# Softmax probabilities turned in 32x32 blocks on VectorE and spread by SBUF to SBUF transfers, in place of TensorE transposes, in a two-block attention kernel

## What is computed

```python
# block 0, q = x, k = v = ctx
qn, kn, vn = _ln(q, ...), _ln(k, ...), _ln(v, ...)
qh, kh, vh = (einsum('btd,hed->bhte', n, W) for n, W in ((qn, Wq), (kn, Wk), (vn, Wv)))
attn = einsum('bhte,bhse->bhts', qh, kh) + rel_bias[idx]
p = softmax(attn / sqrt(HS), axis=-1)
out = einsum('bhts,bhse->bhte', p, vh)
x = q + out.reshape(B, T, H * HS) @ fc_w.T + fc_b
x = x + gelu(_ln(x, ln2_g, ln2_b) @ W1.T + b1) @ W2.T + b2
# block 1, query = x, key = value = ctx
scores = where(|i - j| <= 64, q @ k.T / sqrt(16), NEG)
attn = (softmax(scores) @ v) @ Wo + bo
gate = silu(concat([attn, query]) @ Wg + bg)
out = attn * gate + query * (1 - gate)
x_hat = out * rsqrt(mean(out * out) + EPS) * rms_w
return x_hat - mean(x_hat, axis=1)
```

## Time and profile before

| what | value |
|---|---|
| median of 3 runs | 2212.92 us |
| the profiled execution | 2203.2 us |
| its span, first to last instruction | 2201.5 us |
| PE busy | 2152.8 us, 98% |
| PE weight loads (beside PE) | 1978.8 us, 90% |
| VectorE busy | 1575.8 us, 72% |
| ScalarE busy | 1648.2 us, 75% |
| POOL busy | 891.0 us, 40% |
| mean granted TensorE clock | 0.997 of full speed |
| DMA | 37.36 MB, 32236 packets |

### The profile page before, as it was taken

How to read it: one execution, slowest core, us unless ns; L and a number is a source line. 1 busy time by engine, 2 the same in 40 slices (tenths; PEclk the granted TensorE clock), 3 DMA queues, 4 the chain that set the end, 5 groups by cost and what they waited for, 6 DMA issues and landing times.

```text
span 2201.5 us, 57835 instructions
## 1 busy us (share of the span) xinstructions
PE 2152.8 (98%) x20908; PEld 1978.8 (90%) x20908; DVE 1575.8 (72%) x6779; ACT 1648.2 (75%) x5742; POOL 891.0 (40%) x978
## 2 busy tenths in 40 slices
PE   8999999999999999999999999999999999999985
PEld 8998999999999999999999999999999999999973
DVE  4666777767777767777777777777777776777764
ACT  3677787777787777787777787777777787777774
POOL 1234444434444434444434344434444433444433
PEclk9999999999999999999999999999999999999998
DMA  5000000000000000000000000000000000000000
GB/s 174 11 11 11 16 9 16 14 12 15 16 9 16 14 16 11 16 9 16 14 16 11 16 9 16 14 16 11 16 9 16 14 16 11 16 9 16 4 6 10
DMA packets 32236, 37.36 MB, mean 17 GB/s; under 512 B 2512, under 2 KB 30800, under 8 KB 31952
## 3 DMA queue, kind: packets, MB, share of 16 engines
q1 hardware_dynamic: 31952, 33.67, 4.9%
HBM read 25.27 MB, written 8.39 MB: 15 GB/s over the span
## 4 chain that ended last, share of the span: by engine, by line
PE 96%; DVE 1%; ACT 1%; issue 0%; DMA 0%; POOL 0%; SPq 0%; POOLq 0%; DVEq 0%; ACTq 0%
PE bank L276 20%; PE bank L277 19%; PE bank L278 19%; PE bank L416 6%; PE bank L439 6%; PE bank L536 6%; PE bank L426 5%; PE bank L284 3%; PE bank L549 3%; PE bank L526 3%; PE bank L577 2%; PE bank L357 1%; PE bank L292 1%; PE bank L360 1%; ACT soft L1852 1%
## 5 line engine op out<-in xcount | busy, mean ns | idle before, releaser
L2232 POOL TENSOR_TENSOR soft<-soft,inv_sum 128x512 f32<-128x512 f32 x256 | 266.7, 1042 | 443.9 <-DVE inv_sum L1227 441.5
L1852 ACT ACTIVATE soft<-soft,row_min 128x128 f32<-128x128 f32 x1024 | 396.4, 392 | 48.9 <-DVE row_min L1219 48.7
L1774 ACT ACTIVATE soft<-soft,row_min 128x128 f32<-128x128 f32 x1024 | 398.5, 393 | 34.8 <-DVE row_min L1099 34.0
L2224 POOL TENSOR_TENSOR soft<-soft,inv_sum 128x512 f32<-128x512 f32 x256 | 268.6, 1049 | 268.1 <-DVE inv_sum L1107 264.4
L1099 DVE CUSTOM_DVE_ANT_0 soft<-bank,relb 128x128 f32<-128x128 f32 x1024 | 232.6, 282 | 14.6 <-PE bank L416 12.3
L1219 DVE CUSTOM_DVE_ANT_0 soft<-bank,winb 128x128 f32<-128x128 f32 x1024 | 224.4, 284 | 13.1 <-PE bank L526 13.1
L1852 ACT ACTIVATION_READ_ACCUMULATOR soft<-soft,row_min 128x1 f32 x1024 | 195.4, 191 | 0.0
L1774 ACT ACTIVATION_READ_ACCUMULATOR soft<-soft,row_min 128x1 f32 x1024 | 195.0, 190 | 0.0
L1077 DVE TENSOR_SCALAR kT<-bank,bk 128x256 f32<-128x256 f32 x256 | 111.1, 474 | 106.9 <-PE bank L278 106.7
L1764 ACT ACTIVATE qT<-bank,bq 128x256 f32<-128x256 f32 x256 | 106.2, 467 | 107.1 <-PE bank L278 106.3
L536 PE MATMUL bank<-ident,soft 128*128 128x128 f32 x1024 | 160.3, 280 | 6.2 <-POOL soft L2232 6.2
(11 more groups left out here) (197 smaller groups left out, 7581.7 us busy)
## 6 DMA issues: line engine op xcount, KB each, us to landing
X<-in_x SPq DMA_DIRECT2D x32, 256.0 KB, 2.7
C<-in_ctx SPq DMA_DIRECT2D x32, 256.0 KB, 2.7
out<-gate SPq DMA_DIRECT2D x64, 128.0 KB, 1.7
soft<-in_wv_t SPq DMA_DIRECT2D x2, 512.0 KB, 7.5
softT<-in_w_t SPq DMA_DIRECT2D x2, 512.0 KB, 3.8
rows<-in_rows SPq DMA_DIRECT2D x1, 648.0 KB, 8.8
soft<-in_wq_t SPq DMA_DIRECT2D x1, 512.0 KB, 6.3
softT<-in_wq_t SPq DMA_DIRECT2D x1, 512.0 KB, 7.0
```

The costliest lines, as they stand in the source:

```text
L1774: last = act.activation(soft[:, s, h, :], soft[:, s, h, :], ACT.Exp, bias=row_min[:, s, h:h + 1], scale=-1.0, accum_out=row_sum[:, s, h:h ...
L1852: last = act.activation(soft[:, s, h, :], soft[:, s, h, :], ACT.Exp, bias=row_min[:, s, h:h + 1], scale=-1.0, accum_out=row_sum[:, s, h:h ...
L2224: pool.tensor_tensor(soft[:, m % 2, :, :], soft[:, m % 2, :, :], inv_sum[:, m % 2, :].unsqueeze(2).broadcast_to([P, QUAD, SEQ]), ALU.mult) ...
L2232: pool.tensor_tensor(soft[:, 2 + u, :, :], soft[:, 2 + u, :, :], inv_sum[:, 2 + u, :].unsqueeze(2).broadcast_to([P, QUAD, SEQ]), ALU.mult) ...
```

## The change

It takes the transposes of the probabilities off PE. `turn0` and `turn1` become one VectorE instruction for each unit, which transposes every 32x32 block of the 128x512 unit by itself into the new tile `turned` (three slots: one for block 0, two for block 1). Four transfers of 64 KB from SBUF to SBUF, issued by SP, then carry each group of 32 partitions of `turned` over all 128 partitions, back into the slot of `soft` that the unit came from. For that to be the transpose, the keys stand in another order: `k_out` and `kv_out` write them with a step, and the relative bias and the window mask are laid out to match. `pv` and `pv1` read the probabilities from `soft` in runs of 32. The copies `t0_out` and `t1_out` go, and so does `softT`; `soft` gets four slots for block 0 instead of two. `x_norm`, `c_norm` and `h_norm` move from VectorE to POOL, `hid_hi` from VectorE to ScalarE. NK1 becomes 2. The order of all five engines is written anew, the loop now runs from 4 to NG - 3, the banks are bank 0, bank 1, `ring2` and `ring4`, and `kv_out` of group r is in round r instead of r - 1. The start-up's weight staging uses slots of `soft` where it used `softT`, and the first group's layer norm stands earlier.

```diff
+BLOCK = 32
-        ring1 = banks[1:8]
+        ring2 = banks[2:4]
+        ring4 = banks[4:8]
-        NS, NST = 2 + NU1, 4
+        NS0 = 4
+        NS = NS0 + NU1
         soft = sb("soft", [P, NS, QUAD, SEQ])
-        softT = sb("softT", [P, NST, QUAD, SEQ])
+        NB = SEQ // BLOCK
+        turned = sb("turned", [P, 3, NB, QUAD, BLOCK])
-        NK1 = 3
+        NK1 = 2
...
+        def turn_blocks(eng, slot, s):
+            return eng.transpose(turned[:, slot, :, :, :].rearrange("p j h b -> p h j b"),
+                                 soft[:, s, :, :].rearrange("p h (j a) -> p h j a", j=NB))
+        def spread(eng, s, slot, name):
+            for i in range(NB):
+                eng.dma_start(soft[:, s, i, :], turned[i * BLOCK:(i + 1) * BLOCK, slot, :, :, :]).then_inc(sem[name], 16)
+        def turned_of(s, h):
+            return soft[:, s, :, :].rearrange("p i (h b) -> p i h b", h=QUAD)[:, :, h, :]
...
 sync_program
+            def spread0(g, m):
+                till.wait_ge("turn0", 2 * NQ * g + m + 1)
+                spread(sp, m % NS0, 0, "spread0")
+            def spread1(g, b, u):
+                till.wait_ge("turn1", unit1(g, b, u) + 1)
+                spread(sp, NS0 + u, 1 + u % 2, ("spread1_even", "spread1_odd")[u % 2])
+            for r in range(4, NG - 2):
+                spread0(r, 0)
                 load_x(r + 1)
+                spread0(r, 1)
+                spread0(r, 2)
+                spread1(r - 2, 1, 0)
+                spread1(r - 2, 1, 1)
+                spread0(r, 3)
+                spread1(r - 2, 1, 2)
+                spread1(r - 2, 1, 3)
+                spread0(r, 4)
+                spread0(r, 5)
                 store(r - 2, 0)
+                load_c(r + 2)
+                spread0(r, 6)
+                spread0(r, 7)
+                spread1(r - 1, 0, 0)
                 store(r - 2, 1)
+                spread1(r - 1, 0, 1)
+                spread1(r - 1, 0, 2)
+                spread1(r - 1, 0, 3)
...
 tensor_program: turn0 and turn1 removed; in pv and pv1
-                till.wait_ge("t0_out_s", NQ * g + Q + 1)
-                till.wait_ge("t0_out_v", NQ * g + Q + 1)
+                till.wait_ge("spread0", 16 * NB * 2 * (NQ * g + Q + 1))
-                                         softT[:, slot, h, :], start=True, stop=True)
+                                         turned_of((2 * Q + slot) % NS0, h), start=True, stop=True)
-                till.wait_ge("t1_out_s", GROUP * KD * g + KD * b + n + 1)
-                till.wait_ge("t1_out_v", GROUP * KD * g + KD * b + n + 1)
+                till.wait_ge("spread1_even", 16 * NB * (KD * (GROUP * g + b) + n + 1))
+                till.wait_ge("spread1_odd", 16 * NB * (KD * (GROUP * g + b) + n + 1))
...
 vector_program: t0_out, t1_out, x_norm, c_norm, h_norm and hid_hi removed
                 for c in range(QC):
                     i = Q * QC + c
-                    last = dve.tensor_scalar(kT[:, c, :], bank[:, c * TOK:(c + 1) * TOK], bk[:, i:i + 1], None, ALU.add)
+                    last = dve.tensor_scalar(kT[:, c, :].rearrange("p (b j a) -> p b j a", b=GROUP, j=NB),
+                                             bank[:, c * TOK:(c + 1) * TOK].rearrange("p (b a j) -> p b j a", b=GROUP, j=NB),
+                                             bk[:, i:i + 1], None, ALU.add)
...
-                if n >= 2:
-                    till.wait_ge("turn0", n - 1)
+                if n >= NS0:
+                    till.wait_ge("pv", (n - NS0) // 2 + 1)
...
+            def turn0(g, m):
+                n = 2 * NQ * g + m
+                till.wait_ge("norm0", n + 1)
+                if n > 0:
+                    till.wait_ge("spread0", 16 * NB * n)
+                turn_blocks(dve, 0, m % NS0).then_inc(sem["turn0"], 1)
+            def turn1(g, b, u):
+                n = unit1(g, b, u)
+                till.wait_ge("norm1", n + 1)
+                if n >= 2:
+                    till.wait_ge(("spread1_even", "spread1_odd")[u % 2], 16 * NB * (n // 2))
+                turn_blocks(dve, 1 + u % 2, NS0 + u).then_inc(sem["turn1"], 1)
...
 scalar_program: t0_out and t1_out removed
+            def hid_hi(g, half):
+                till.wait_ge("gelu", 2 * g + half + 1)
+                if g + half > 0:
+                    till.wait_ge("w2", 4 * g + 2 * half)
+                act.copy(flat(hidS[:, HI, :, :]), flat(hid[:])).then_inc(sem["hid_hi"], 1)
...
 gpsimd_program
+            def x_norm(g):
...
+                for b in range(GROUP):
+                    last = pool.tensor_scalar(normed[:, b, :], X[:, g % 2, b, :], moments[:, b, 0:1], rstd[:, b:b + 1],
+                                             ALU.subtract, ALU.mult)
+            def c_norm(g):
+            def h_norm(g):
```

More of the change, by code:

```diff
@@ L188, in sync_program, with weight_in @@
             till = Till(sp)
-            def weight_in(slot, src):
+            def weight_in(slot, src, *read):
+                for name, count in read:
+                    till.wait_ge(name, count)
                 buf = stage[slot]
@@ L418, in scores @@
                 last.then_inc(sem["scores"], 1)
-            def turn0(g, m, bank, *drains):
-                if not there(g):
-                    return
-                freed(till, *drains)
-                till.wait_ge("norm0", 2 * NQ * g + m + 1)
-                for h in range(QUAD):
-                    last = pe.transpose(bank[:, h * SEQ:(h + 1) * SEQ], soft[:, m % 2, h, :], ident[:])
-                last.then_inc(sem["turn0"], 1)
             def pv(g, Q, bank, *drains):
@@ L528, in scores1 @@
                 last.then_inc(sem["scores1"], 1)
-            def turn1(g, b, u, bank, *drains):
-                if not there(g):
-                    return
-                freed(till, *drains)
-                till.wait_ge("norm1", unit1(g, b, u) + 1)
-                for h in range(QUAD):
-                    last = pe.transpose(bank[:, h * SEQ:(h + 1) * SEQ], soft[:, 2 + u, h, :], ident[:])
-                last.then_inc(sem["turn1"], 1)
             def pv1(g, b, n, bank, *drains):
@@ new lines, in vector_program @@
+            turn1(1, 0, 3)
+            inv0(3, 1)
+            turn0(3, 0)
+            x1_sum(2, banks[7])
+            min0(3, 2, banks[6])
+            stats2_(2)
+            min0(3, 3, banks[1])
+            moments2_(2)
+            k_out(3, 2, banks[3])
+            var2(2)
+            inv0(3, 2)
+            turn0(3, 1)
+            o1_lo(1, 0, banks[2])
+            min1(1, 1, 0, banks[1])
+            min1(1, 1, 1, banks[6])
+            min1(1, 1, 2, banks[7])
+            inv1(1, 1, 0)
@@ new lines, in vector_program @@
+            min1(1, 1, 3, banks[0])
+            turn0(3, 2)
+            turn1(1, 1, 0)
+            inv1(1, 1, 1)
+            inv0(3, 3)
+            h_lo(2, banks[2])
+            v_out(3, 1, banks[6])
+            inv1(1, 1, 2)
+            o_lo(3, 0, banks[1])
+            turn1(1, 1, 1)
+            min0(3, 4, banks[7])
+            inv1(1, 1, 3)
+            ag_sum(1, 0, banks[3])
+            turn0(3, 3)
+            turn1(1, 1, 2)
+            stats0(4)
+            gate_(1, 0)
+            inv0(3, 4)
@@ new lines, in vector_program @@
+            turn1(1, 1, 3)
+            moments0(4)
+            min0(3, 5, banks[0])
+            turn0(3, 4)
+            hid_lo(2, 0)
+            k_out(3, 3, banks[3])
+            var0(4)
+            inv0(3, 5)
+            o_lo(3, 1, banks[2])
+            mean_sq(1, 0)
+            v_out(3, 2, banks[3])
+            kv_out(3, banks[4])
+            turn0(3, 5)
+            o1_lo(1, 1, banks[7])
+            x_hat(1, 0)
+            hid_lo(2, 1)
+            min0(3, 6, banks[3])
+            min0(3, 7, banks[0])
@@ new lines, in vector_program @@
+            moments0(NG - 1)
+            min0(NG - 2, 5, banks[0])
+            turn0(NG - 2, 4)
+            hid_lo(NG - 3, 0)
+            k_out(NG - 2, 3, banks[2])
+            var0(NG - 1)
+            inv0(NG - 2, 5)
+            o_lo(NG - 2, 1, banks[3])
+            mean_sq(NG - 4, 0)
+            v_out(NG - 2, 2, banks[2])
+            kv_out(NG - 2, banks[7])
+            turn0(NG - 2, 5)
+            o1_lo(NG - 4, 1, banks[6])
+            x_hat(NG - 4, 0)
+            hid_lo(NG - 3, 1)
```

2404 lines of the change are left out of this document (1377 added, 1027 removed).

## The result

The changed kernel takes 2234.28 us in the median of its runs (2227.81 to 2241.23), the kernel before 2212.11 (2210.83 to 2213.86): a ratio of 1.010, 95% interval 1.0068 to 1.0133. It is slower by 1%, where 2007 us and 9% faster were forecast. The profiled execution took 2241.23 us, its span is 2239.5.

A forecast was written before the change was run, and what follows sets the result against it. PE's work was taken to bound the rounds: 2203.2 us - 232 (transposes) + 12 (tail) + 14 (waits) = 1997, plus 9.7 from profiled execution to median, gave 2007 us. Its own range was 1955 to 2045; 8 in 10, 1955 to 2120.

The forecast's parts named there:

- TensorE's transposes: On PE: removing 512 groups of four transposes saves 232 us (ends 225 and 240), 7.25 us a round.
- the tail: At the kernel's end: about four softmax units in a row, each taking 4.2 instead of 1.1 us, +12 us.
- waits in the rounds: In 28 steady rounds: allowance of 0.5 us each for a fuller VectorE and longer ways, +14 us.
- In the rounds PE's other products hide that: In the rounds: PE's other products cover the 4.2 us from a unit's turn to its product, helped by four layer 0 slots.
- a unit's way: From a unit's turn to its product: turn 0.69, four issues of 0.46, landing 1.7, together 4.2 us, against 1.1 before.
- R4: Rival: loop through layer 0's one buffer and SP's queue, 5.5 + 64 i + 8 L a round, about 2500 us; chance 0.09.
- The block transpose: On VectorE: one 128x512 block transpose takes 0.69 us, between 0.4 and 1.21, 16 a round, 11.0 us.
- R1: Rival: VectorE becomes the bound if block transposes are held up or take 1.21 us, about 2100 us; chance 0.10.
- R3: Rival: runs of 32 slow the moving operand of the probability products; 2209 us if doubled, 2057 at a quarter more; chance 0.05.
- ScalarE's cast of the hidden layer: On ScalarE: 64 added casts of 1.045 us each, 67 us in all.
- POOL's tensor-scalar: On POOL: 192 added 128x256 normalisations at 735 ns, 4.4 us a round, 32.1 in all.
- R2: Rival: PE waits 0.5 us for late spreads at each of 8 products, +4 us a round, about 2120 us; chance 0.11.

The follow-up runs named there:

- e6: Changed kernel without any spreading transfer, nothing waiting for a landing, output left out of account: 2048.15 us.
- e5: Changed kernel with two 128 KB transfers per unit instead of four of 64 KB, rows landing in wrong places: 2059.86 us.
- e1: Changed kernel with the three turned buffers serving all sixteen units of a round in rotation: 2141.28 us.
- e9: Changed kernel with layer 1's units spread two at a time by four 128 KB transfers, layer 0 as it was: 2206.79 us.
- e14: Changed kernel with two turned buffers for layer 0 and one for layer 1: 2539.16 us.
- e15: Kernel before without TensorE's transposes of the probabilities, copies reading them untransposed from SBUF, output left out of account: 2174.40 us.
- e2: Changed kernel with only the normalisation of C moved back from POOL to VectorE: 2203.55 us.
- e17b: e1 with three products that wait for spreads (two of layer 0, one of layer 1) one step later in TensorE's order: 2192.92 us.
- e18b: e1 with only the two layer 0 products that wait for spreads one step later in TensorE's order: 2149.22 us.
- e10: e9 with the three buffers handed out so that each unit or pair takes those used longest ago: 2147.26 us.
- e12: Layer 0's units spread in pairs by four 128 KB transfers, layer 1's singly, buffers oldest first, against the changed kernel: 2337.18 us.

## Why the prediction was wrong

Against the profiled execution's 2203.2 us the terms came out so, by the round of the changed kernel (66.14), of e6 (60.40) and of before (65.81), and by what of each span lies outside of 32 rounds (95.6 us before, 123.0 after):

| term | forecast | measured |
|---|---|---|
| TensorE's transposes | -232 | (60.40 - 65.81) x 32 = -173 |
| the tail (measured: both ends) | +12 | +27 |
| waits in the rounds | +14 | (66.14 - 60.40) x 32 = +184 |
| sum | 1997 | 2241 |

**The step that failed is the allowance for waits**, 14 us, that is 0.5 us in each of 28 rounds, where 184 were measured. Behind it stands the sentence "In the rounds PE's other products hide that", said of a unit's way. It took the way for a latency that runs beside PE. It is a link of a loop: the turn waits for the landing, VectorE's queue stands behind the turn, PE's banks behind VectorE. e5 and e6 show the size (174 and 186 us), e1 that 93 of them are the assignment of the buffers alone. Of the 5.74 us a round, 4.55 are idle time of PE (from 400 to 1600 us it is idle 5.26 us a round, in e6 0.71). The other 1.2 are PE's own work, which takes longer: the mean granted clock there is 0.99, with short stretches at the lower of its two levels, and 1.00 in e6. How much of the 1.2 the clock makes was not separated.

**R4 was the right rival, at a chance of 0.09.** Its mechanism is in the profile as it was written, but that SP is not busy without rest: VectorE waits for the landing and SP waits for VectorE. Its prices were too low: I took 0.46 us for an issue from a store and a load that follow each other, and the store's 1.7 us for a landing. A spread's issue follows the one before by 0.645 us and lands in 2.14. With these R4's formula as written gives 5.5 + 64 x 0.645 + 8 x 2.14 = 63.9 us, against 66.14 measured. That it comes near is luck. A landing is counted from the start of its issue, so the formula, like the 4.2 us of a unit's way in the prediction, counts one issue of each unit of layer 0 twice; without them it gives 58.7 us, less than e6's round. And as a sum it is not the law: e9, with 16 issues fewer, should have fallen by 10 us and fell by 1.3, and e14, with the same count of everything, rose by 9.4. What is missing is how close the units come that share a buffer, and that they queue for SP in bursts.

**TensorE's term** was too high by 59 us. Of these, 23 are the 0.7 us a round that PE still waits in e6; its work alone fell by 65.81 - 59.69 = 6.1 us a round, and in e15 by 65.8 - 60.2 = 5.6. The spacing in the earlier trace rows, 0.47 - 0.12 = 0.35 us a group, is 5.6 us a round; the 0.09 us that I added for the longer matmul behind a group, and the chain's 240 us, made the term too high. A 128x256 product lasts longer behind other kinds too (median 0.39 us behind `pv` or `scores` in e6, 0.28 behind its own kind, 0.36 behind the transposes before), so much of that cost stays when the transposes go. In the old order most of the term could not even be had (e15).

**The tail and start** cost 27 us instead of 12; 20 of them are there without any transfer (e6: 2048.5 - 32 x 60.40 = 115.7, against 95.6), so they come with the new order, which I had not priced; e15, in the old order, has 97.7. Which part of the new order they are is not shown. The granted clock over the last 139.5 us is 0.74, where it was 0.92 in the last 101.5 before; PE is idle there for 42% of the time.

**Point by point.** The block transpose was right: 703 ns, within 668 to 717, and R1 did not come true: no run shows VectorE as the bound (68% busy). R3 was right to be small: the same product takes 279 ns in e1 and 286 (L595) over the changed kernel, where L439 had 279. ScalarE's cast of the hidden layer takes 1.05 us, as forecast. POOL's tensor-scalar takes 1.23 to 1.25 us, not 0.735, so POOL has 34.8 us a round instead of 32.1; harmless as a sum, but 2.44 us of it lie in the loop (e2, without them, is 31 us faster). DMA packets took 32.2% x 2239.5 x 16 / 326864 = 35 ns each, below the 54 taken as an upper estimate. R2, PE waiting for late spreads, is in the trace (50.2 + 79.9 us, 4.1 a round, the 4 us that R2 had named), but it is the loop's end as seen from PE, not a cause of its own: e17b and e18b move it without a gain.

What remains open: why single issues take up to 2.16 us (the maximum in the row of L187), why a load takes longer behind spreads, and what a fourth buffer of `turned` would give. The last was not tried.

## What to carry to other kernels

A transfer put between two in-order engines is not a latency beside the work but a link in a loop: write the loop down (turn, issues, landing, what waits for the buffer, what is queued behind that wait), and compare the time between two units that share a buffer with the time that one holds it, before counting any engine's busy time. Price an issue by its own kind in a run of its kind, never by another kind's. Fewer, larger transfers are worth a try: an issue cost the same 0.6 us for 64 and for 128 KB. But the 174 us of e5 are an upper end, as its rows land in the wrong places; the versions that keep the result with fewer issues (e9, e10, e12) did not beat e1. Buffers shared in rotation beat buffers tied to a stage, and were the cheapest part to change: 93 us for the same work and the same memory.

## What the runs showed that I had not expected

- An issue of an SBUF to SBUF transfer takes SP 603 ns and 645 from start to start, whatever it holds (591 ns with rows of 2 KB, 606 with 128 KB), where a store and a load in a row came 0.46 us apart. A load behind spreads pays nearly as much (592 ns, 368 without spreads), and so does ScalarE's queue (626 ns).
- POOL's tensor-scalar with two per-partition scalars takes 1249 ns for 128x256 (the normalisation of C), the tensor-tensor of the same size 735; on VectorE the same normalisation took 547.
- How three buffers are handed out moves the time from 2141 us (in rotation, e1) over 2234 (one for layer 0, two for layer 1) to 2539 (two and one, e14), with the same work on every engine.
